# First attention of a two-layer block: products with V in groups of four steps, V kept once, eight buffers of probabilities

## The reference

```python
q = (x @ Wq).reshape(B, S, H, D).transpose(0, 2, 1, 3)      # 16 heads of 64, x after layer norm
k = (c @ Wk).reshape(B, N, D, H).transpose(0, 3, 2, 1)
v = (c @ Wv).reshape(B, N, D, H).transpose(0, 3, 1, 2)
mask = jnp.all(c == 0, axis=-1)[:, None, None, :]
scores = jnp.einsum('bhsd,bhdn->bhsn', q, k) * scale
scores = jnp.where(mask, -jnp.inf, scores)
att = jax.nn.softmax(scores, axis=-1)
out = jnp.einsum('bhsn,bhnd->bhsd', att, v)
return out.transpose(0, 2, 1, 3).reshape(B, S, H * D) @ Wo
```

## Time and profile before

| | us |
|---|---|
| median of 3 runs | 2121.53 (2121.21 to 2129.98) |
| the profiled execution | 2127.05 |
| its span, first to last instruction | 2125.3 |
| TensorE busy | 1982.3 (93%) |
| VectorE busy | 1693.7 (80%) |
| ScalarE busy | 1065.4 (50%) |
| GpSimd busy | 1161.7 (55%) |
| products with V (L479), 3328 matmuls | 405.2 |

### The profile page before, as it was taken

The page is one execution under the profiler, slowest core; times in us unless marked ns, Lnnn a source line. Parts: engine busy times, 40 slices in busy tenths (PEclk is TensorE's granted clock), DMA queues, the critical chain, the costliest instruction groups (busy, mean ns, idle before and its releaser), DMA issues. The chain is left out here.

```text
span 2125.3 us, 35171 instructions
## 1 busy us (share of the span) xinstructions
PE 1982.3 (93%) x10757; PEld 1451.8 (68%) x10757; DVE 1693.7 (80%) x4048; ACT 1065.4 (50%) x1493; POOL 1161.7 (55%) x624
## 2 busy tenths in 40 slices
PE   5999999999999999999999999999966899779995
PEld 4677777777677777767777777777645688557774
DVE  7898888888887888888888888888647777757765
ACT  3445445453545545453545545454534799644442
POOL 0275756657575655757575666657764445314340
PEclk9899999999999999999999999999986999879997
DMA  3000000000000000000000000000000212112210
GB/s 95 1 1 17 1 4 17 1 1 4 18 1 4 2 16 1 4 18 1 1 4 17 1 4 1 1 1 1 1 6 16 91 60 75 38 49 63 74 35 24
DMA packets 54855, 40.84 MB, mean 19 GB/s; under 512 B 2500, under 2 KB 51596, under 8 KB 53644
## 3 DMA queue, kind: packets, MB, share of 16 engines
q1 hardware_dynamic: 54668, 38.57, 6.1%
HBM read 37.45 MB, written 1.11 MB: 18 GB/s over the span
## 5 line engine op out<-in xcount | busy, mean ns | idle before, releaser
L374 POOL TENSOR_TENSOR a_den<-a_den,a_probs 128x1024 f32<-128x1024 f32 x352 | 844.3, 2402 | 332.2 <-ACT a_probs L572 331.8
L572 ACT ACTIVATE a_probs<-a_probs,a_mask_col 128x1024 f32<-128x1024 f32 x416 | 478.8, 1151 | 571.8 <-DVE a_probs L741 571.7
L741 DVE TENSOR_TENSOR a_probs<-a_scores,a_shift 128x512 f32<-128x512 f32 x832 | 565.0, 685 | 160.1 <-PE a_scores L399 138.8
L682 DVE CUSTOM_DVE_ANT_0 a_work<-a_work,a_mask_row 128x400 f32<-128x400 f32 (+1 forms) x1024 | 571.7, 589 | 47.7 <-PE a_work L431 47.3
L479 PE MATMUL a_pv<-a_probs,a_V 128*64 128x256 f32 x3328 | 405.2, 385 | 1.0 <-ACT a_probs L572 0.9
L397 PE MATMUL a_scores<-a_Q_hi,a_cT_hi 128*128 128x512 f32 x832 | 345.7, 415 | 6.4 <-DVE a_probs L741 4.6
L431 PE MATMUL a_work<-a_cT_hi,a_Q_hi 128*128 128x400 f32 (+1 forms) x1024 | 328.0, 369 | 2.4
L398 PE MATMUL a_scores<-a_Q_lo,a_cT_hi 128*128 128x512 f32 x832 | 328.1, 394 | 0.0
L399 PE MATMUL a_scores<-a_Q_hi,a_cT_lo 128*128 128x512 f32 x832 | 326.6, 393 | 0.0
L479 PEld LDWEIGHTS a_pv<-a_probs,a_V 128*64 128x64 f32 x3328 | 220.5, 136 | 150.3 <-issue 39.1
L431 PEld LDWEIGHTS a_work<-a_cT_hi,a_Q_hi 128*128 128x128 f32 x1024 | 193.7, 190 | 98.3 <-issue 43.1
(11 more groups left out here) (319 smaller groups left out, 2849.4 us busy)
## 6 DMA issues: line engine op xcount, KB each, us to landing
m_gate_rows<-gate_scratch SPq DMA_DIRECT2D x8, 1024.0 KB, 4.9
a_c_nat<-in_ctx_dram SPq DMA_DIRECT2D x8, 768.0 KB
b_c_in<-in_ctx_dram SPq DMA_DIRECT2D x8, 768.0 KB
b_c_nat<-in_ctx_dram SPq DMA_DIRECT2D x8, 768.0 KB
m_w_raw<-in_L_ffn_W_dram SPq DMA_DIRECT2D x16, 256.0 KB, 5.0
a_acc<-in_x_dram SPq DMA_DIRECT2D x8, 128.0 KB, 2.1
out_dram<-tokens SPq DMA_DIRECT2D x4, 256.0 KB, 2.3
a_V<-in_L_xattn_Wq_dram SPq DMA_DIRECT2D x1, 512.0 KB, 6.6
```

The lines of the kernel that those rows point to most:

```text
L374: nc.gpsimd.tensor_tensor(half, so_far, probs[:, buffer(c, j), :], ALU.add).then_inc(den_added, 1)
L572: nc.scalar.activation(probs[:, buffer(c, j), :], probs[:, buffer(c, j), :], ACT.Exp, bias=mask_col[:, c // 2 % 2, j // 2:j // 2 + 1]).the ...
L682: nc.vector.tensor_tensor_reduce(out=X[:, bank, :w], in0=X[:, bank, :w], in1=mask_row[:, off:off + w], scale=1.0, scalar=-3e38, op0=ALU.ad ...
L741: nc.vector.tensor_tensor(probs[:, buffer(c, j), pair * 2 * S:(pair + 1) * 2 * S], Sc[:, pair, :], shift[:, first:first + 2 * S], ALU.add) ...
```

## The change

The products with V are done for four steps at once (at j = 3, 7, ... 23, and the last two steps at 25), so 32 matmuls of the trace in a row and 7 groups in a stage. V is kept once: chunk i for the next stage is computed behind the group that was the last to read chunk i of this one, two chunks behind each group, and ScalarE waits for those products ahead of its copy. The `early` list has only Q and the maxima (68 items in even stages, 76 in odd ones), spread over the same slots. There are eight buffers of probabilities for four. The raw weights lie where the one copy of V is.

```diff
@@ -118,8 +118,21 @@
     BANKS = 4
     TAIL = 3
 
-    V_AFTER = [1, 4, 6, 8, 10, 12, 14, 26, 38]
-    LATE_V = [95, 97, 100, 102]
+    BUFFERS = 8
+    GROUP = 4
+
+    def group_ends(j):
+
+        return j % GROUP == GROUP - 1 or j == STEPS - 1
+
+    def group_of(j):
+
+        return range(j - j % GROUP, j + 1)
+
+    def v_slot(chunk):
+
+        end = next(j for j in range(2 * chunk + 1, STEPS) if group_ends(j))
+        return 4 * end + 2 + chunk % 2
     MAX_END = 92
     SHIFTS = [83, 93]
     DIAG = [84, 88]
@@ -135,11 +148,7 @@
         if group == 0:
             early += [("cT", i) for i in range(3)] + [("cxT", 3)] + [("mask", i) for i in range(4)]
         early += [("q", i) for i in range(4)]
-        vs = [("v", c) for c in range(NC)]
-        for u in range(UNITS * 4):
-            early.append(("max", u))
-            if u in V_AFTER:
-                early.append(vs.pop(0))
+        early += [("max", u) for u in range(UNITS * 4)]
         slots = [[] for _ in range(SLOTS)]
         for n, item in enumerate(early):
             slots[n * MAX_END // len(early)].append(item)
@@ -149,9 +158,8 @@
             slots[DIAG[i]].append(("diag", i))
         for i in range(4):
             slots[SPREAD[i]].append(("spread", i))
-        assert len(vs) == len(LATE_V)
-        for n, item in zip(LATE_V, vs):
-            slots[n].append(item)
+        for chunk in range(NC):
+            slots[v_slot(chunk)].append(("v", chunk))
         return slots
 
     CONTEXT_ITEMS = 4
@@ -201,11 +209,11 @@
 
         c_nat = sb("c_nat", [P, NC, D])
         cT = [[sb(f"cT_{part}{i}", [P, NC * P], F32R) for part in ("hi", "lo")] for i in range(2)]
-        V = sb("V", [P, 2, NC, G8 * HD])
+        V = sb("V", [P, NC, G8 * HD])
         Q = [[sb(f"Q_{part}{i}", [P, G8 * S], F32R) for part in ("hi", "lo")] for i in range(2)]
         shift_diag = sb("shift_diag", [P, UNITS // 2, P], F32R)
         shift = sb("shift", [P, G8 * S])
-        probs = sb("probs", [P, 4, 4 * S])
+        probs = sb("probs", [P, BUFFERS, 4 * S])
         den = sb("den", [P, G8 * S])
         G = [sb("G_hi", [P, H, D], F32R), sb("G_lo", [P, H, D], F32R)]
         Wv = [sb("Wv_hi", [P, H * HD], F32R), sb("Wv_lo", [P, H * HD], F32R)]
@@ -226,7 +234,7 @@
         ones_b = sb("ones_b", [P, P], BF16)
         ones_r = sb("ones_r", [P, P], F32R)
 
-        raw = [V[:, 1, :, :].rearrange("p c n -> p (c n)")[:, i * 1024:(i + 1) * 1024] for i in range(6)]
+        raw = [V[:, :, :].rearrange("p c n -> p (c n)")[:, i * 1024:(i + 1) * 1024] for i in range(6)]
         wq_raw, wk_raw, wv_raw, wk_heads, wqT, wkT = raw
         squares = probs[:, 0:2, :].rearrange("p a (t d) -> p (a t) d", d=D)
 
@@ -303,7 +311,7 @@
 
         def buffer(c, j):
 
-            return (c * STEPS + j) % 4
+            return (c * STEPS + j) % BUFFERS
 
 
         @block.sync
@@ -477,7 +485,7 @@
                     cols = (j % 2 * 2 + pair) * S
 
                     last = nc.tensor.matmul(PV[HD * odd:HD * odd + HD, cols:cols + S],
-                                            V[:, c % 2, j // 2, h * HD:(h + 1) * HD],
+                                            V[:, j // 2, h * HD:(h + 1) * HD],
                                             probs[:, buffer(c, j), (pair * 2 + odd) * S:(pair * 2 + odd + 1) * S],
                                             start=(j < 2 and pair == 0), stop=(j >= STEPS - 2), skip_group_check=True)
                 if pair == 1:
@@ -488,11 +496,11 @@
                 slots = the_plan(it, c)
                 for j in range(STEPS):
                     for part in range(4):
-                        if part == 1 and j % 2 == 1:
-
-                            for both in (j - 1, j):
-                                pv(it, c, both, 0)
-                                pv(it, c, both, 1)
+                        if part == 1 and group_ends(j):
+
+                            for step in group_of(j):
+                                pv(it, c, step, 0)
+                                pv(it, c, step, 1)
                         elif part > 1 and j + 2 < STEPS:
                             qk(it, c, j + 2, part - 2)
                         elif part > 1 and prep:
@@ -553,7 +561,10 @@
                     nc.scalar.activation(Q[s % 2][0][:, i * 512:(i + 1) * 512], X[:, bank, :], ACT.Copy)\
                       .then_inc(hi_done, 1)
                 elif kind == "v":
-                    nc.scalar.activation(V[:, s % 2, i, :], X[:, bank, :], ACT.Copy).then_inc(bank_free[bank], 1)
+                    if c >= 0:
+
+                        act.wait_ge(pv_done, steps_of(it, c, 2 * i + 2))
+                    nc.scalar.activation(V[:, i, :], X[:, bank, :], ACT.Copy).then_inc(bank_free[bank], 1)
                 elif kind == "spread":
                     if c >= 0:
 
@@ -732,10 +743,11 @@
 
                         for quarter in (2 * j, 2 * j + 1):
                             taken(dve, it, prep_use(it, c - 1, "spread", quarter))
-                    if c > 0 or j > 3:
-
-                        dve.wait_ge(pv_done, steps_of(it, c, j - 3))
-                        added = 1 if j == 4 else 2 if j == 5 else j - 5 if j > 5 else j - 3
+                    if c > 0 or j >= BUFFERS:
+
+                        last = j - BUFFERS
+                        dve.wait_ge(pv_done, steps_of(it, c, last + 1))
+                        added = last + 1 if last in (0, 1) or last < 0 else last - 1
                         dve.wait_ge(den_added, at(it, 4 * (STEPS - 2), c * (STEPS - 2) + added))
                 first = (j % 2 * 4 + pair * 2) * S
                 nc.vector.tensor_tensor(probs[:, buffer(c, j), pair * 2 * S:(pair + 1) * 2 * S],
```

## The result

The changed kernel takes 2244.32 us (2240.45 to 2255.25, 4 runs) against 2123.48: 1.057 times as long, interval 1.053 to 1.062. The forecast was 2187, at most 2223. The way was right, the size was not: +121 us for +65.

What follows compares the result with a forecast made beforehand. TensorE sets stage length on average, VectorE close behind and binding early. Seven even stages at +5.1, seven odd at +4.0, stage 0 at +1.5 and the last at 0 give +65 us: 2187, range 2118 to 2223.

Steps and rivals of the forecast that it cites:

- Less switching: Stages 0 to 14: 13 groups become 7, saving 0.35 us of TensorE switching each, 2.1 us a stage, 31 us in all.
- The last stage: Stage 15: what is saved in switching is lost in turns of the score bank, 10.42 us against 10.40; entered as 0.
- VectorE bound early: Slots 5 to 28: VectorE has 23.3 us of work in even stages; TensorE owes more at slot 29, +2.4 even, +1.8 odd.
- nothing ahead of it gets faster, so it stays: Stage 10: the first maximum still starts 10.9 us after the group at slot 101.
- Stall in the middle: Cycles of 16 slots: TensorE waits for VectorE after a group of 32, 0.75 us a cycle, 3.0 us a stage.
- Odd stages: Seven odd stages: +1.8 early, +3.0 for middle stalls, -0.8 for small waits that go, +4.0 us each.
- Eight buffers and one copy of V: VectorE's waits for GpSimd go but it then waits for scores; ScalarE's copies of V are covered: 0 for each.
- carry its lead through: Rival, TensorE bound throughout: its lead absorbs the uneven feeding and the 31 us come out, 2088 us; 15%.
- Only the early part bound: Rival: middle stalls stay near 0 and only the early part of stages is bound, +20 to +35, 2142 to 2157 us; 15%.
- The wash: Rival: turns and waits eat exactly what less switching saves, 2121 us within 10; 10%.

Runs made afterwards that it cites:

- short reciprocals: Changed kernel with the eight reciprocals of each stage cut from 128 to 8 columns, leaving most out: 2188.91 us; the same in the kernel before: 2107.04 us.
- groups of two with the like remedies: Changed kernel with groups of two steps, reciprocals spread from slot 13, first half of the shift at slot 77, fourth item of Q in slot 3: 2127.22 us, 0.9995.

## Why the prediction was right or wrong

The spans grew by 118 us for the 65 forecast. Of the 53 missing, 26 lie in the seven odd stages, 15 in the seven even ones, 6 in the preparation and stage 0, the rest in the last stage and in single stages.

*Less switching, 2.1 us a stage: right as far as it shows.* A group of 32 takes 1126.50 - 1122.89 = 3.61 us up to the next matmul, as 1.87 + 1.72 said.

*The last stage, 0: right.* Groups in its middle are 10.44 us apart (10.42 forecast).

*VectorE bound early: right in kind; the time at slot 29 of even stages came out by luck.* The 23.3 us of work are there: from the first maximum at 1119.49 to the end at 1142.7 it is 23.2. One step failed: "nothing ahead of it gets faster, so it stays". The first maximum came 12.2 us behind the group at slot 101, not 10.9. The longer spacing of the shorter list had moved the fourth item of Q from slot 3 to slot 4, which puts its copy behind the exp of step 2 on ScalarE. I had counted the maxima in the new list and not gone through it for what each item stands behind; with the item put back the 10.9 returned. Yet in an even stage without a fall of the clock the group at slot 29 comes 32.9 us behind that at slot 101, for 32.7 forecast. Stage 2, timeline of TensorE:

```profile
280.34 1.95 PE L487 MATMUL a_pv<-a_probs,a_V 128*64 128x256 f32 x16
313.20 3.67 PE L487 MATMUL a_pv<-a_probs,a_V 128*64 128x256 f32 x32
```

Two other errors made up for the late start: VectorE had none of the 0.5 us of short waits, and TensorE's group came 2.5 us before VectorE was through and not 2.0. In stage 10 VectorE keeps to the same times, but the group comes 33.7 us behind: the 0.9 is the fall of the clock.

*Stall in the middle, 0.75 us in every cycle: mis-sized, and this is the step of the sum that failed in every stage.* Against TensorE's own 12.9 us the last three cycles of stage 10 take 13.94, 13.74 and 14.81: 1.0, 0.8 and 1.9. The first two are near. The third holds the first half of the shift, in the very chain of VectorE's work that TensorE waits for. I had no term for it; moved to the group, it gave 0.85 us back, 0.54 of them being the minimum's wait for GpSimd. In both kinds of stage this cycle costs 1.1 us more than forecast, 16 us in all.

*Odd stages, +4.0: mis-sized.* They paid 7.7, and this is the largest part of the miss, 26 us over seven stages: 14.2 us for a middle cycle (13.2 own, with 13 maxima), 15.1 with the shift, and 1.4 for 0.3 early. The maxima are denser there, and I had entered the same 0.75 for both. About 1 us of the 3.7 has no name. The early part has a like cause as in even stages, seen in the timeline of VectorE, stage 11 of the kernel before and then of the changed one:

```profile
1136.35 1.29 DVE L643 TENSOR_TENSOR a_Q_lo<-a_work,a_Q_hi 128x512 fp32r<-128x512 f32 x2 [0.36 <-ACT a_Q_hi L553]
```

```profile
1228.47 0.69 DVE L654 TENSOR_TENSOR a_Q_lo<-a_work,a_Q_hi 128x512 fp32r<-128x512 f32 x1 [0.84 <-ACT a_Q_hi L561]
1230.22 0.69 DVE L654 TENSOR_TENSOR a_Q_lo<-a_work,a_Q_hi 128x512 fp32r<-128x512 f32 x1 [1.05 <-ACT a_Q_hi L561]
```

With 76 items for 85 the third and fourth item of Q moved to slots 12 and 13, and TensorE comes to the fourth only behind the group of 32 (at 1228.58, the group at 1224.97); VectorE stands idle for 1.9 us there, where it lost 0.4 before. That this is the 1.1 us too much is read from the rows; no run moved Q in odd stages.

*Eight buffers and one copy of V, 0: not tested apart.* With groups of two they cost 21 us together with the new order of items, and nothing is left of it once reciprocals, shift and Q have better places. A few us of cost could hide behind what those places gave.

*The rivals.* TensorE did not carry its lead through: with 31 us less switching its waits grew by more. "Only the early part bound" fell too, since short reciprocals left 61 us of loss. The wash missed by more than 100 us; it is where the kernel came to stand only after the reciprocals, the shift, V, Q and the maxima had been moved.

## What to carry to other kernels

When a group of matmuls feeds nobody for 3.6 us, the engine behind it loses that time, and the matmuls then wait for it. Work that needs no matmul (here reciprocals, the shift) belongs beside the group; here that made the loss good, and no run came out ahead by the 31 us of switching. An engine that is busy for 80 to 85% of a stage can bind it through its place in the order, so add up its work between two fixed points and not over the stage. When a list is spread anew, follow every item to its slot and see what it now stands behind in each queue.

## What the runs showed of the hardware

**A small operation of VectorE waits for GpSimd.** The minimum on 128 x 8 elements at L709 (L698 before), by its instructions; first the kernel before, then the changed one, then the reduction in its place.

```profile
L698 DVE TENSOR_SCALAR a_neg_max<-a_neg_max x32: 171/289/401, 71.1 to 1492.8; 128x8 f32<-128x8 f32 x32
```

```profile
L709 DVE TENSOR_SCALAR a_neg_max<-a_neg_max x32: 170/760/920, 74.9 to 1609.8; 128x8 f32<-128x8 f32 x32
```

```profile
L709 DVE TENSOR_REDUCE a_neg_max<-a_neg_max x32: 160/161/165, 74.2 to 1601.3; 128x8 f32<-128x8 f32 x32
```

The columns are shortest, median and longest in ns. It takes 0.17 us in both kernels when no addition of GpSimd runs beside it and 0.28 us or more in each case when one does; the timeline of all engines in stage 10 shows one such case.

```profile
1193.17 4.72 POOL L382 TENSOR_TENSOR a_den<-a_den,a_probs 128x1024 f32<-128x1024 f32 x2 [3.81 <-ACT a_probs L583]
...
1194.63 0.18 DVE L704 TENSOR_REDUCE a_neg_max<-a_maxes 128x8 f32<-128x32 f32 x1
1194.84 0.75 DVE L709 TENSOR_SCALAR a_neg_max<-a_neg_max 128x8 f32<-128x8 f32 x1
```

The first of the two additions ends at about 1195.5, and so does the minimum, while the reduction just ahead of it is not slowed. The Trainium skill (Perfetto Trace Analysis, Optimizing Scalar/DVE Operations) says that GpSimd and VectorE share a read port of SBUF, and that a VectorE operation which uses two ports holds it as an exclusive lock. The rows fit a lock, here with GpSimd as the holder and 0.75 us for 0.17 as the price; that the port is the reason they can't show. In groups of two with the like remedies the minimum took up to 2.11 us.

**TensorE's clock fell in a stage that was bound by VectorE.** Windows of the changed kernel, ahead of the fall, during it and behind it:

```profile
1132.20:1137.40 5.20, 3.01 (x11) 1.53 (x10) 5.20 (x14) 1.15 (x1) 3.17 (x2) 1.00 0.00 0
1137.40:1140.80 3.40, 3.30 (x8) 2.34 (x8) 3.40 (x10) 1.15 (x1) 3.40 (x2) 0.51 0.00 0
1140.80:1144.00 3.20, 3.20 (x30) 2.02 (x30) 1.88 (x6) 1.15 (x1) 3.20 (x3) 0.99 0.00 0
```

TensorE had been busy for 3.01 of 5.20 us when the granted clock fell from 2.4 to 1.2 GHz. Between 90 and 1560 us this happened nine times in the changed kernel, never in the one before, and once with short reciprocals. Where it did, the stretch from slot 13 to 29 of an even stage took 18.15 us or a little more, elsewhere 17.27: 0.9 us each, some 8 us in all. The forecast had no term for it.
